# A graph attention layer: the one-hot of the lanes by a comparison of two tensors in place of a comparison with a scalar

## The reference

```python
recv = edge_index[:, 0]; send = edge_index[:, 1]
n_in = node[recv]; n_out = node[send]
wn_out = n_out @ W_lin + b_lin
e_ij = leaky_relu2(concatenate([n_in, n_out], -1) @ W_att + b_att)
a_ij = (e_ij @ w_alpha)[:, 0]
seg_max = segment_max(a_ij, recv)
a_exp = exp(a_ij - seg_max[recv])
alpha = a_exp / maximum(segment_sum(a_exp, recv)[recv], 1e-12)
n_i = segment_sum(alpha[:, None] * wn_out, recv)
x = layernorm(x + elu(n_i))
```

## Time and profile before

| | before |
|---|---|
| median of three runs | 2303.85 us |
| span of the profiled execution | 2302.9 us |
| POOL busy | 1626.4 us, 71% |
| DVE busy | 1753.5 us, 76% |
| PE busy | 1790.7 us, 78% |
| ACT busy | 1463.3 us, 64% |
| one-hot (L1529) | 415 times, 487 ns mean |
| gather (L650) | 1635 times, 978 ns mean |

### The profile page before, as it was taken

One profiled execution on the slowest core, in us unless ns is written; L12 is line 12 of the kernel. 1 busy time (PEld: TensorE's weight loads), 2 busy tenths in 40 slices (PEclk: granted clock), 3 DMA queues, 4 the chain that ended last, 5 costly groups with the idle time before them and its releaser, 6 DMA issues.

```text
span 2302.9 us, 62793 instructions
## 1 busy us (share of the span) xinstructions
PE 1790.7 (78%) x11498; PEld 1460.1 (63%) x11705; DVE 1753.5 (76%) x5214; ACT 1463.3 (64%) x4913; POOL 1626.4 (71%) x1670
## 2 busy tenths in 40 slices
PE   4658788877878888887878787878888788787770
PEld 2337676766667666766666666666666666666660
DVE  9849887877789787786888787878766666666667
ACT  2327687876667666665666666666666666666665
POOL 2067777777777777777777777777777777777760
PEclk9769999999999999998999999999899999999995
DMA  3145555555455555554555555555555555555541
GB/s 120 60 113 136 133 136 131 132 128 140 127 134 131 134 132 133 132 136 127 131 131 130 127 136 134 132 131 129 132 138 135 135 134 135 133 135 134 132 111 56
DMA packets 165719, 294.14 MB, mean 128 GB/s; under 512 B 40002, under 2 KB 110014, under 8 KB 165329
## 3 DMA queue, kind: packets, MB, share of 16 engines
q0 software_dynamic: 78864, 216.03, 36.8%
q1 hardware_dynamic: 85733, 73.82, 13.0%
q10 hardware_dynamic: 732, 0.27, 0.1%
HBM read 278.95 MB, written 11.02 MB: 126 GB/s over the span
## 4 chain that ended last, share of the span: by engine, by line
POOL 22%; issue 12%; PE 10%; DMA 7%; DVE 3%; DVEq 1%; ACT 0%; POOLq 0%; ACTq 0%
POOL rows L650 22%; DMA rows<-qv_table,senders 7%; PE masked_ps L977 3%; PE hidden_ps L966 2%; PE turned_ps L992 2%; PE hidden_ps L964 2%; PE turned_ps L984 1%; DVE sums L1579 1%; DVE spare L1670 0%; DVE leaky L1535 0%; PE masked_ps L976 0%; DVEq L1579 0%; DVE x_sb L1665 0%; ACT x_sb L853 0%; DVE sums L1655 0%
## 5 line engine op out<-in xcount | busy, mean ns | idle before, releaser
L650 POOL DMA_INDIRECT rows<-qv_table,senders x1635 | 1598.4, 978 | 498.3 <-issue 465.7
L964 PE MATMUL hidden_ps<-identf,rows 128*128 128x128 f32 x1635 | 466.4, 285 | 311.4 <-DMA rows<-qv_table,senders 298.6
L1579 DVE SCALAR_TENSOR_TENSOR sums<-sums,shrink,turned_ps 128x129 f32 x1660 | 571.2, 344 | 81.3 <-issue 26.9
L992 PEld LDWEIGHTS turned_ps<-rows,spare 128*128 128x128 f32 x3270 | 439.0, 192 | 299.8 <-ACT spare L777 212.4
L762 ACT ACTIVATE spare<-masked_ps,peaks 128x128 f32<-128x128 f32 x1660 | 472.8, 368 | 218.6 <-DVE peaks L1557 216.9
L966 PE MATMUL hidden_ps<-onehotT,p_unit 128*128 128x128 f32 x3320 | 602.4, 284 | 0.0
L1542 DVE TENSOR_REDUCE lows<-masked_ps 128x4 f32<-128x512 f32 x415 | 285.8, 689 | 401.2 <-PE masked_ps L977 399.6
L966 PEld LDWEIGHTS hidden_ps<-onehotT,p_unit 128*128 128x128 f32 x3320 | 531.7, 201 | 0.9 <-issue 0.9
L992 PE MATMUL turned_ps<-rows,spare 128*128 128x129 f32 x3270 | 473.0, 279 | 60.8 <-DVE sums L1579 54.6
L752 ACT ACTIVATE sloped<-hidden_ps 128x512 f32<-128x512 f32 x415 | 249.2, 600 | 345.7 <-PE hidden_ps L966 342.6
L964 PEld LDWEIGHTS hidden_ps<-identf,rows 128*128 128x128 f32 x1635 | 239.2, 146 | 356.2 <-issue 332.1
(11 more groups left out here) (201 smaller groups left out, 865.6 us busy)
## 6 DMA issues: line engine op xcount, KB each, us to landing
lanes_all<-lane_list SPq DMA_DIRECT2D x415, 128.0 KB
single_rows<-qv_table SPq DMA_DIRECT2D x3200, 1.0 KB
rows<-qv_table,senders POOLq DMA_INDIRECT x1635
qv_table<-rows SPq DMA_DIRECT2D x24, 257.0 KB, 2.7
out<-x_sb SPq DMA_DIRECT2D x1, 1344.0 KB
out<-x_sb SPq DMA_DIRECT2D x1, 896.0 KB
kept<-windows SPq DMA_DIRECT2D x3, 208.0 KB
out<-x_sb SPq DMA_DIRECT2D x1, 448.0 KB
```

Source lines behind the costliest of these rows:

```text
L650: g.indirect_dma_start(out=rows[:, k % U, c, :], out_offset=None, in_=table, in_offset=bass.IndirectOffsetOnAxis(ap=senders[:, s % 2, c * ...
L964: t.matmul(whole[:, unit], rows_at_unit(k, c)[:, 0:F], identf[:], is_transpose=True, start=True, stop=False, skip_group_check=True)
L992: mm = t.matmul(unit_sums_ps[:, c, :], weights[:, k % 2, c * P:(c + 1) * P], rows_at_unit(k, c)[:, F:R], start=True, stop=True)
L1579: v.scalar_tensor_tensor(out=at, in0=at, scalar=shrink[:, k % 4, i:i + 1], in1=unit_sums_ps[:, i, :], op0=ALU.mult, op1=ALU.add).then_inc( ...
```

## The change

The one-hot is the result of the same comparison, lanes equal to the partition's number, with the same input tile, output tile, type, semaphores and place in the program. Before, the partition's number was a scalar operand of a tensor_scalar, one value per partition. Now the instruction is a tensor_tensor with two tensor inputs: the lanes (bf16, 512 a partition) and `part_f` (f32, one value a partition) spread along the free axis by a step of zero.

```diff
@@ -1526,7 +1526,8 @@
                 dve.wait_ge(lanes_in[k % LANE_RING], (k // LANE_RING + 1) * 16)
                 if k >= 4:
                     dve.wait_ge(masked_done, k - 3)
-                v.tensor_scalar(onehotT[:, k % 4, :], lanes_all[:, k % LANE_RING, :], part_f[:], None, ALU.is_equal).then_inc(onehotT_ready, 1)
+                v.tensor_tensor(onehotT[:, k % 4, :], lanes_all[:, k % LANE_RING, :], part_f[:].to_broadcast([P, CHUNK]),
+                                ALU.is_equal).then_inc(onehotT_ready, 1)
 
             def leaky_relu(k):
```

## The result

The changed kernel takes 2355.35 us, the median of five runs (2353.46 to 2364.52), against 2305.96 us for five of the kernel before. The ratio is 1.0223, 95% interval 1.0205 to 1.024: 49 us slower. The forecast had the direction and the mechanism; its +24 us were half of what came, and 2355 lies above its range, which ended at 2348.

The account below looks back on a forecast made before the run. POOL's back-to-back gathers were taken as the bound: 28 us of stretching removed, 50 to 53 us added, DVE's extra 85 us free, so 2303.85 + 24 = 2328 us. The range was 2304 to 2348 us, held with 0.8.

Parts of the forecast that it names:

- What bounds the kernel: POOL's 1635 indirect gathers run without a stop; 52 us in which they last longer than needed change the time one for one.
- DVE's 82 us cost nothing: On DVE: 415 one-hots, 0.205 us longer each, add 85 us of busy time, which by themselves cost nothing.
- A tensor_tensor holds a gather at its start, until its end plus 0.82 us; not in the middle: DVE beside POOL's gathers: read from the padding comparison, six of ten over a gather's start, agreeing to 0.01 us.
- The removed part: POOL's gathers: stretching by the old tensor_scalar one-hot that goes away, 25.5 + 2.8 = 28 us.
- The added part: POOL's gathers: new holds by the 0.691 us tensor_tensor, at the start only, worked out three ways; coupled 50 and 53 us.
- the coupled run: Third estimate: one-hots keep their distance from the gathers that fed them; old 27 and 28 us, new 50 and 53.
- the fixed starts: First estimate: one-hot starts left where they are; 200 gathers caught, 58 us, net +30.
- its rule: A DVE operation begun before a gather and running 0.125 us into it delays it until its end, then 0.82 us are left.
- a start caught at least 0.05 us early: Second estimate, starts spread alike over the 1.25 us period: mean delay 0.106 us, x 415 = 44 us, net +26.
- The sort's conflicts: Gathers stretched by DVE operations other than the one-hot, 24 of the 52 us, fall anew: 5 us either way.
- The sum: Whole kernel: 2303.85 + 24 = 2328 us, the +24 taken from the third, coupled way of counting.
- the second pattern: A one-hot beginning 0.35 to 0.5 us into a gather stops it until 0.12 us after its end; 45 gathers, 2.8 us.

Follow-up runs that it names:

- the run with 821 ns a one-hot: The one-hot as the tensor_scalar of the kernel before, with an accumulator output to a scratch column added: 2275.5 us against 2303.3 for before, ratio 0.9881.

## Why the prediction was wrong

- **What bounds the kernel.** Right. POOL's gathers, back to back, with gaps of 0.30 us before and after, carry 49.0 of the 50.7 us, and in all eight profiles the span follows the stretched gathers within 4 us.
- **DVE's 82 us cost nothing.** Right: POOL never waited, and the run with 821 ns a one-hot is 28 us faster than before.
- **A tensor_tensor holds a gather at its start, until its end plus 0.82 us; not in the middle.** Right: 180 gathers, 56.0 us, and none held in the middle. The inference in the Trainium skill's "SBUF — State Buffer", section "Who interferes with whom", that a tensor_tensor leaves GpSimd's descriptors alone, does not hold here, with these 180 gathers. The Trainium skill's rule in the same section, that an instruction with two SBUF inputs contends with a GpSimd instruction that reads SBUF, agrees with them. The Trainium skill's exception there for the tensor_scalar that also writes out its accumulator agrees too, with 948 ns in 231 gathers.
- **The removed part.** Right: 28 us worked out, and the run in which the one-hot holds nothing won 27.8 us. The table has 31.5, because 16 of its 48 gathers held in the middle, with 4.6 us, had been held at their start by a sort operation first.
- **The added part failed.** This is the step that failed. I took 50 to 53 us from the coupled run; it is 69.0. Of the difference, 3 to 6 us are the ordinary conflicts (56.0, close to the 58 of the fixed starts), and 13.0 are a term that the forecast put at nothing: its rule wants an operation that began before the gather, and its estimate "a start caught at least 0.05 us early". That limit came from the tensor_scalar: of nine of its one-hots that began from less than 0.05 us before to 0.02 us after a gather's start, none held the gather. Of 13 tensor_tensors there, eight did. These and two that begin up to 0.14 us after the start make up less than half of the term. The rest, 7.3 us, are the nine gathers behind the sort's 91-partition operations. The rule lets a gather be served as soon as the operation that holds it ends, and here the next one went on holding it. The trace of before had two gathers, at 1142.12 and 1166.12, that can be read so already. This is the first, with the timelines of DVE and POOL before. By the rule it would be served when the first sort operation ends, at 1142.45, and end at 1143.27, and the one-hot would begin too late to stop it. It ends at 1143.64, 0.12 us behind the one-hot, as the rule has it for a gather served only behind the second sort operation, at 1142.79:

```profile
1142.03 0.42 DVE L1150 TENSOR_TENSOR keys<-keys 91x256 f32<-91x256 f32 x1
1142.37 0.42 DVE L1151 TENSOR_TENSOR keys<-keys 91x256 f32<-91x256 f32 x1
1142.71 0.34 DVE L1579 SCALAR_TENSOR_TENSOR sums<-sums,shrink,turned_ps 128x129 f32 x1
1142.97 0.15 DVE L1567 TENSOR_TENSOR growth<-peaks 128x4 f32<-128x4 f32 x1
1143.04 0.48 DVE L1529 TENSOR_SCALAR onehotT<-lanes_all,part_f 128x512 f32<-128x512 bf16 x1
...
1142.12 1.52 POOL L650 DMA_INDIRECT rows<-qv_table,senders  x1 [0.30 <-issue]
```

- **The sort's conflicts, "5 us either way".** They cost 6.1 us more, and all else 5.6 us: 3.5 of these are the gathers up to 0.96 us, whose median is 3 ns longer, and the rest falls on other operations. Why they fell so is not shown.
- **The sum.** Forecast: 50 to 53 for 28, rounded to +24. Measured: 69.0 - 31.5 = 37.5 from the one-hot, 6.1 from the sort, 5.6 from the rest: 49.2 us. The mechanism of single holds was right; the added conflicts were taken too small, and holds by two operations in a row were missing.
- **The range.** Its upper end came from the case in which the tensor_tensor shows the second pattern too, +45 and so 2349 us; the range was then written as ending at 2348. The sort's 5 us either way were left out of it, and it had no room for terms that come together.

## What to carry to other kernels

Where one engine issues without a gap, look at the spread of its instruction's duration, not only at its waits: here 52 us stood in no idle column. A DVE instruction beside a GpSimd that issues gathers is judged by how many SBUF inputs it has and whether it runs in the fast form, then by how long one instruction lasts, and only last by DVE's busy time: the form with 821 ns beat those with 487 and 685. Where such an instruction can't be avoided, cutting it in two helps (2316 against 2355 us here). A rule read from one form of an instruction gives the other form's mechanism, but its limits have to be read again there, and conflicts that depend on phase want a wide upper end.

## What the runs showed of the hardware that was not expected

- An accumulator output takes a tensor_scalar from 487 to 739 ns plus 82 ns for the read, and takes away every hold on the gathers (948 ns mean under it).
- Two tensor_tensors of 256 columns hold gathers for 34.7 us in sum, one of 512 for 69.0.
- A gather that begins as a two-input operation on 91 partitions ends, or under one, can be held through a two-input operation that begins 0.25 to 0.5 us into it (1.76 and 2.01 us). On 128 partitions the same places, counted where the operation ends as the gather begins, give 0.94 to 1.17 us. Why a part of the partitions does this is open. So is why about ten other gathers of the changed kernel were held by a one-hot that began from 0.05 us before to 0.14 us after their start. No run has one input of the one-hot in PSUM; that such an instruction leaves gathers alone is shown by the leaky relu's maximum (949 ns).
